# Expert outputs of an AdaLN attention + MoE block: six stored rows per token against four accumulator rows added by the scatter

## The chip, the core and the metric

The kernel runs on one core of a Trainium2 chip, in one launch. The metric is the device time in microseconds from the first to the last instruction of the core. Everything is float32 unless said otherwise. Engines are called PE (matrix multiply; PEld is its weight load), DVE (vector), ACT (scalar), POOL (GpSimd) and SP (the queue that issues most transfers).

## The reference

One transformer block on `x` of shape (8, 256, 256): adaptive layer norm, gated linear attention with ternary weights, residual, a second adaptive layer norm, and then a mixture of experts with a shared expert. Only the last part touches the change:

```python
# 2048 tokens, E = 64 experts, TOPK = 6 per token, H = 256, F = 96
pos  = position of the (token, expert) choice within its expert
valid = pos < CAP                       # CAP = 48 places per expert
buf[expert, pos] = h[token]             # choices past CAP are dropped
out  = (silu(buf @ w_gate) * (buf @ w_up)) @ w_down      # per expert
y[token] = sum over its valid choices of out[expert, pos] * weight
x = x + gb * (y + shared(h))
```

Of 12288 choices at most 64 x 48 = 3072 are valid; the others add nothing to `y`.

## The kernel before

**Token stage.** For each of 8 batches (256 tokens, two tiles of 128) the five engines run a software pipeline, `step(s, ...)` under `token_steps`: norms, attention, router, shared expert. Its result per batch is `pre` (residual plus gated shared expert, kept in SBUF) and a dispatch: POOL scatters each token's row, with its 64 expert weights and some keys, by `slot_ix` to memory (`rows_dram`, 64 experts x 64 slots, L449), 12 indirect transfers a batch. Beside it ACT issues one transfer per batch that fills an eighth of `y_dram` with zeros (L578), since most of its 12288 rows (six per token) are never written.

**Pair stage.** The 64 experts go two at a time, 32 pairs, under `pair_steps`. A pair is 128 slot rows: SP loads the rows of two pairs per transfer (L346) and, for pairs 0 to 15, behind them the weights of two later pairs (`load_quad`, L321 to L323; pairs 0 to 15 had theirs loaded in the token stage). PE transposes the rows (L1257), multiplies gate and up (L1268), transposes (L1275) and multiplies down (L1281). ACT does the tanh (L625), a copy, and the weighted evacuation of the down product into one of OBUF = 4 buffers `e_out` (the halves of `oT` and `osq`; L545 with `wcol`). DVE copies the transposed rows (L984), does the two products (L989, L992), copies the pair's weights (L1001), and works out for each slot row its place in `y_dram`: token times 6 plus the rank of this expert among the token's (`larger`, `rank`, `y_row`; L1003 to L1008). POOL then scatters the 128 rows by `y_row` to `y_dram` (`put`, L494), 1 KB a row; rows of empty slots get an index out of bounds and are left out.

After scatter q POOL waits for the landing of scatter q-3 and then raises `e_free` (L500), which ACT waits for ahead of an evacuation into a used buffer. So up to four scatters are under way.

**Last stage.** When all scatters have landed, SP reads `y_dram` in 16 tiles of 128 tokens, six rows (6 KB) per token (L366), through YBUF = 4 buffers. DVE sums six rows by a reduction (L1019); POOL multiplies by the gate `gb_all` (L516) and adds `pre` (L521), each behind a tiny `settle` instruction (L439); SP stores the tile (L370).

## Time and profile before

| | |
|---|---|
| median of 3 runs | 516.87 us (515.25 to 517.76) |
| profiled execution, first to last instruction | 517.1 us |
| token stage, about | 0 to 374 us |
| pair stage | 374 to 464 us |
| last stage | 464 to 517 us |
| busy over the span | PE 60%, DVE 55%, POOL 41%, ACT 19% |

The profiled execution is as long as the timed ones, so nothing lies around its span that a sum would have to add. The busy shares are averages over three stages with different limits: PE does nothing in the last 53 us, and DVE and POOL little in the pair stage. What the change does has to be read stage by stage.

### The profile page before, as it was taken

How to read it: one execution, taken by the hardware profiler on the slowest of the kernel's cores; microseconds unless marked ns; L12 is line 12 of the kernel's file. 1: busy time of each engine (PE TensorE's matmuls, PEld its weight loads, DVE VectorE, ACT ScalarE, POOL GpSimd, SP SyncE). 2: the span in 40 equal slices, each digit the busy share in tenths (PEclk: the TensorE clock that was granted, in tenths of full speed). 3: DMA queues.
4: the chain of work that ended last, by engine and by line, in shares of the span. 5: the costliest groups of instructions: out<-in, count | busy, mean ns of one | idle time of the engine just before them, and what ended most of it. 6: DMA issues, size and time to landing. Idle time of an engine off the chain costs nothing.

```text
span 517.1 us, 7330 instructions
## 1 busy us (share of the span) xinstructions
PE 309.6 (60%) x2282; PEld 222.4 (43%) x2282; DVE 283.7 (55%) x1066; ACT 98.9 (19%) x253; POOL 212.8 (41%) x310
## 2 busy tenths in 40 slices
PE   0735695968678768859657867150089889940000
PEld 0424484856556556747445655040045444520000
DVE  3550516395194394393393392664067544727995
ACT  1411131413112212303113201000024332430000
POOL 4200112117517527327327237186615433553664
PEclk9958568896786886796787787655579865985555
DMA  7955992963411311311301300000059999119992
GB/s 224 399 183 178 260 317 71 239 214 127 171 35 61 125 47 47 122 41 39 122 20 38 122 22 8 0 5 2 3 153 300 277 270 228 57 38 379 333 323 96
DMA packets 62332, 73.63 MB, mean 142 GB/s; under 512 B 9458, under 2 KB 56955, under 8 KB 62304
## 3 DMA queue, kind: packets, MB, share of 16 engines
q1 hardware_dynamic: 41456, 53.37, 35.2%
q10 hardware_dynamic: 14704, 15.24, 8.4%
q0 software_dynamic: 6144, 4.66, 3.1%
q8 instruction: 15, 0.25, 0.2%
q14 instruction: 13, 0.11, 0.1%
HBM read 48.39 MB, written 40.93 MB: 173 GB/s over the span
## 4 chain that ended last, share of the span: by engine, by line
issue 27%; PE 19%; DVE 16%; POOL 15%; DMA 10%; another core or an unknown queue 5%; ACT 3%; SPq 2%; DVEq 1%; ACTq 0%; POOLq 0%
POOL rows_dram L449 8%; PE ps_s L1268 5%; DVE z L1019 4%; DMA h2row<-rows_dram 2%; DVE scm L821 2%; DMA xa<-in_L_attn_x 2%; DMA scm<-rows_dram 2%; DMA egu<-y_dram 2%; POOL rstd L435 2%; PE ps_o L1166 2%; SPq L300 1%; PE ps_o L1281 1%; PE ps_a L1257 1%; PE ps_c L1281 1%
## 5 line engine op out<-in xcount | busy, mean ns | idle before, releaser
L449 POOL DMA_INDIRECT rows_dram<-h2row,slot_ix x96 | 94.3, 983 | 28.1 <-issue 28.1
L435 POOL TENSOR_TENSOR rstd<-ve,half_exp 128x2 f32<-128x2 f32 x15 | 11.2, 743 | 133.6 <-DVE ve L662 133.4
L1019 DVE TENSOR_REDUCE z<-egu 128x256 f32<-128x1536 f32 x16 | 42.7, 2746 | 10.8 <-DMA egu<-y_dram 10.8
L439 POOL TENSOR_TENSOR pool_pad<-half_exp 128x1 f32<-128x1 f32 x72 | 13.7, 191 | 68.4 <-ACT oT L545 17.0
L821 DVE TENSOR_TENSOR scm<-ps_s,decay 128x2048 f32<-128x2048 f32 x16 | 36.6, 2285 | 4.9 <-PE ps_s L1146 4.9
L1268 PE MATMUL ps_s<-egu,attn 128*64 128x192 f32 x256 | 33.7, 391 | 0.1
L1078 PE MATMUL ps_a<-hT,w_qkv 128*128 128x256 f32 x64 | 24.6, 551 | 11.9 <-ACT hsq L569 7.1
L1174 PE MATMUL ps_a<-ident,h2row 128*128 128x128 f32 x32 | 8.9, 435 | 36.7 <-POOL h2row L473 36.7
L1166 PE MATMUL ps_o<-scm,v_eo 128*32 128x128 f32 x512 | 26.8, 357 | 5.6 <-DVE scm L821 5.6
L827 DVE TENSOR_SCALAR r_den<-r_exp 128x128 f32<-128x128 f32 x8 | 1.8, 230 | 44.0 <-issue 35.0
L545 ACT ACTIVATE h2T<-ps_a 128x512 f32<-128x512 f32 x8 | 4.8, 597 | 105.5 <-PE ps_a L1174 105.5
L1078 PEld LDWEIGHTS ps_a<-hT,w_qkv 128*128 128x128 f32 x64 | 16.9, 278 | 15.7 <-issue 12.4
L1268 PEld LDWEIGHTS ps_s<-egu,attn 128*64 128x64 f32 x256 | 18.7, 158 | 7.7 <-issue 2.5
L1174 PEld LDWEIGHTS ps_a<-ident,h2row 128*128 128x128 f32 x32 | 5.7, 217 | 37.7 <-POOL h2row L473 37.7
L1129 PE MATMUL ps_c<-w_proj,oT 128*128 128x256 f32 x64 | 17.2, 415 | 7.4 <-issue 3.8
L1166 PEld LDWEIGHTS ps_o<-scm,v_eo 128*32 128x32 f32 x512 | 16.8, 138 | 11.1 <-issue 10.4
L1193 PE MATMUL ps_c<-h2T,ws_gu 128*96 128x256 f32 x64 | 21.4, 495 | 0.0
L625 ACT ACTIVATE z<-ps_s 128x96 f32<-128x96 f32 x32 | 8.0, 251 | 66.3 <-PE ps_s L1268 63.1
L1101 PE MATMUL ps_c<-w_qkv,hT 128*128 128x256 f32 x64 | 20.6, 480 | 0.0
L1146 PE MATMUL ps_s<-qT,k_eo 32*128 32x128 f32 x512 | 20.2, 297 | 0.0
L1257 PE MATMUL ps_a<-ident,h2row 128*128 128x128 f32 x16 | 4.6, 377 | 25.8 <-DMA h2row<-rows_dram 25.8
L494 POOL DMA_INDIRECT y_dram<-oT,y_row x16 | 15.9, 994 | 9.3 <-POOL pool_pad L439 5.1
(212 smaller groups left out, 725.3 us busy)
## 6 DMA issues: line engine op xcount, KB each, us to landing
y_dram<-y_zeros ACTq DMA_DIRECT2D x8, 1536.0 KB
egu<-y_dram SPq DMA_DIRECT2D x16, 768.0 KB, 5.9
egu<-in_L_ffn_w_gate SPq DMA_DIRECT2D x16, 384.0 KB, 6.7
egu<-in_L_ffn_w_up SPq DMA_DIRECT2D x16, 384.0 KB, 7.9
ed<-in_L_ffn_w_down SPq DMA_DIRECT2D x16, 384.0 KB, 9.7
rows_dram<-scm SPq DMA_DIRECT2D x1, 5376.0 KB, 15.8
mod_b<-mod_dram SPq DMA_DIRECT2D x8, 384.0 KB
h2row<-rows_dram SPq DMA_DIRECT2D x8, 336.0 KB
```

Source lines behind the costliest of these rows:

```text
L435: g.tensor_tensor(out_, in_, half_exp[:, which], ALU.pow).then_inc(S[done], 1)
L449: g.indirect_dma_start(out=rows_dram, out_offset=bass.IndirectOffsetOnAxis(ap=slot_ix[par][:, tile, j:j + 1], axis=0), in_=h2row[par][:, t ...
L494: g.indirect_dma_start(out=y_dram, out_offset=bass.IndirectOffsetOnAxis(ap=y_row[w][:, 0:1], axis=0), in_=e_out[n], in_offset=None, bounds ...
L821: v.tensor_tensor(scm[:].rearrange("p r j q t -> p (r j q t)"), ps_s[:].rearrange("p r n -> p (r n)"), decay[:].rearrange("p r j q t -> p ...
L1019: v.tensor_reduce(ysum[m % NT], y_in[m].rearrange("p (j c) -> p c j", c=C), AX_X, ALU.add).then_inc(S["y_sum"], 1)
L1078: last = mm.matmul(ps_a[:, N * j:N * j + N], w_qkv[:, k, P * j:P * j + P], hT[:, k], start=(k == 0), stop=(k == KC - 1))
L1101: last = mm.matmul(ps_c[:, C * i:C * i + C], hT[:, k, T * i:T * i + T], w_qkv[:, k, 2 * C:3 * C], start=(k == 0), stop=(k == KC - 1))
L1129: last = mm.matmul(ps_c[:, C * i:C * i + C], oT[:, i, k], w_proj[:, k], start=(k == 0), stop=(k == KC - 1))
L1146: last = mm.matmul(ps_s[:, r, col:col + T], k_eo[q][32 * r:32 * r + 32, j, ts], qT[32 * r:32 * r + 32, j, ts], start=True, stop=True)
L1166: last = mm.matmul(dst[32 * r:32 * r + 32], vq, scm[:, r, j, q], start=(q == 0 and not tile), stop=(q == 1), skip_group_check=True)
L1193: last = mm.matmul(ps_c[0:F, N * g_:N * g_ + N], ws_gu[:, k, g_], h2T[:, k], start=(k == 0), stop=(k == KC - 1))
L1268: last = mm.matmul(e_gups[n][rows].rearrange("p (g f) -> p g f", f=F), xt[n][:, k, rows], egu[:, slot // 2, :, 2 * (slot % 2) + half, k], ...
```

## The change

`y_dram` becomes two arrays (`TURNS = 2`) of 2 x 2048 token rows each, plus 128 spare rows. Pair q scatters into array q mod 2; its first expert into that array's first 2048 rows, its second expert into the other 2048 (`side_base`). So the rows of one scatter never meet, and the scatter adds to memory (`compute_op=ALU.add`) in place of writing. A token now has four rows to sum. The place of a row is its token number plus an offset, one DVE instruction in place of three, and the eight keys from which the rank was worked out go: a slot row is 324 numbers in place of 336. Rows of empty slots go to the 128 spare rows (the minimum with `no_token`), one for each partition.

Two scatters into one array could meet in a row, so scatter q is issued only when scatter q-2 has landed.

The last stage is rebuilt: no ring of buffers, all eight batches have their own place in SBUF (six in `egu`, one each in `scm` and `decay`), 32 loads of 256 KB are issued at once, for even batches by SP and for odd ones by ACT. DVE does all arithmetic, four instructions a batch; POOL has no part. Each batch is stored whole.

```diff
-TKEY = KEYS + 8
-ROWW = 336
-YROWS = B * N * TOPK
+TKEY = KEYS
+ROWW = 324
+TOKENS = B * N
+TURNS = 2
+SIDES = 2 * TURNS
+YROWS = 2 * TOKENS
+FAR = 16384
...
-        y_dram = nc.dram_tensor("y_dram", [YROWS, C], F32, kind="Internal").ap()
+        y_dram = [nc.dram_tensor(f"y_dram{i}", [YROWS + P, C], F32, kind="Internal").ap() for i in range(TURNS)]
...
-            for t in range(YBUF):
-                load_y(t, t)
-            with sp.Fori(0, B * NT // YBUF - 1) as i:
-                for m in range(YBUF):
-                    sp.wait_ge(S["y_sum"], YBUF * i + (m + 1))
-                    load_y(YBUF * i + (m + YBUF), m)
-                    store_out(YBUF * i + m, m % NT)
...
+            for b in range(0, B, 2):
+                for a in range(SIDES):
+                    sp.dma_start(y_in[b][:, a], y_v[a // 2][a % 2, b]).then_inc(S[f"ld_y{b}"], 16)
+            for b in range(B):
+                sp.wait_ge(S["y_out"], b + 1)
+                sp.dma_start(out_t[b], y_in[b][:, 0]).then_inc(S["st_out"], 16)
...
+            def put(q):
+                n = q % OBUF
                 pool.wait_ge(S["put_row"], q + 1)
                 pool.wait_ge(S["e_evac"], q + 1)
                 seen(pool, S["put_step"], q)
                 settle(2).then_inc(S["put_step"], 1)
...
-                    pool.wait_ge(S[f"st_put{(n + 1) % OBUF}"], last_n)
+                before_it = q - TURNS
+                if before_it >= 0:
+                    pool.wait_ge(S[f"st_put{before_it % OBUF}"], 16 * (before_it // OBUF + 1))
                     pool.sem_inc(S["e_free"], 1)
...
+                g.indirect_dma_start(out=y_dram[q % TURNS], out_offset=bass.IndirectOffsetOnAxis(ap=y_row[q % WBUF][:, 0:1], axis=0),
+                                     in_=e_out[n], in_offset=None, bounds_check=last_y, oob_is_err=True,
+                                     compute_op=ALU.add).then_inc(S[f"st_put{n}"], 16)
...
-                    a.dma_start(fill_v[s], spread(y_zeros[:], 1, N * TOPK // P)).then_inc(S["st_fill"], 16)
+                    for i in range(TURNS):
+                        a.dma_start(fill_v[i][s], spread(y_zeros[:], 1, 2 * N // P)).then_inc(S["st_fill"], 16)
...
+            def load_y():
+
+                for n in range(OBUF):
+                    act.wait_ge(S[f"st_put{n}"], 16 * PAIRS // OBUF)
+                for b in range(1, B, 2):
+                    for i in range(SIDES):
+                        a.dma_start(y_in[b][:, i], y_v[i // 2][i % 2, b]).then_inc(S[f"ld_y{b}"], 16)
...
-                    v.tensor_tensor(larger[:], xr[x][:, KEYS:TKEY], spread(slot_key[:, q + 1], 1, 8),
-                                    ALU.is_gt).then_inc(S["wcol_ready"], 1)
...
+                    v.tensor_scalar(y_row[w][:], xr[x][:, TKEY:TKEY + 1], side_base[:, 0:1], no_token[:, 0:1],
+                                    ALU.add, ALU.min).then_inc(S["put_row"], 1)
...
+            for b in range(B):
+                dve.wait_ge(S[f"ld_y{b}"], 16 * SIDES)
+                v.tensor_tensor(y_in[b][:, 0:2], y_in[b][:, 0:2], y_in[b][:, 2:4], ALU.add).then_inc(S["y_sum"], 1)
+                dve.wait_ge(S["y_sum"], 2 * b + 1)
+                v.tensor_tensor(y_in[b][:, 0], y_in[b][:, 0], y_in[b][:, 1], ALU.add).then_inc(S["y_sum"], 1)
+                dve.wait_ge(S["y_sum"], 2 * b + 2)
+                v.tensor_tensor(y_in[b][:, 0], y_in[b][:, 0], spread(gb_all[:, b], 1, NT), ALU.mult).then_inc(S["y_gb"], 1)
+                dve.wait_ge(S["y_gb"], b + 1)
+                v.tensor_tensor(y_in[b][:, 0], y_in[b][:, 0], pre[:, NT * b:NT * b + NT], ALU.add).then_inc(S["y_out"], 1)
```

POOL's instructions in the middle of the pair stage, before: a row is line, operation, names, shape, and the semaphores that it waits for. `st_put0` to `st_put3` count the landings of the scatters by buffer.

```order
L439 TENSOR_TENSOR pool_pad<-half_exp 128x1 [waits put_step,e_evac,put_row]
L494 DMA y_dram<-oT,y_row 12288x256
L490 REGISTER_ALU [waits st_put1]
L439 TENSOR_TENSOR pool_pad<-half_exp 128x1 [waits put_step,e_evac,put_row]
L494 DMA y_dram<-oT,y_row 12288x256
L490 REGISTER_ALU [waits st_put2]
```

The same place in the changed kernel, the first four scatters:

```order
L431 TENSOR_TENSOR pool_pad<-half_exp 128x1 [waits e_evac,put_row,st_fill]
L492 DMA y_dram<-oT,y_row 4224x256
L431 TENSOR_TENSOR pool_pad<-half_exp 128x1 [waits put_step,e_evac,put_row]
L492 DMA y_dram<-oT,y_row 4224x256
L431 TENSOR_TENSOR pool_pad<-half_exp 128x1 [waits put_step,e_evac,put_row]
L492 DMA y_dram<-osq,y_row 4224x256 [waits st_put0]
L431 TENSOR_TENSOR pool_pad<-half_exp 128x1 [waits put_step,e_evac,put_row]
L492 DMA y_dram<-osq,y_row 4224x256 [waits st_put1]
```

The wait for a landing has moved from behind a scatter, where it named the scatter three before, to ahead of it, where it names the scatter two before.

DVE's last stage before is a loop of reductions over four buffers:

```order
L1018 ISA [waits ld_y0]
L1019 TENSOR_REDUCE z<-egu 128x256 [waits y_gb]
L1018 REGISTER_ALU [waits ld_y1]
L1019 TENSOR_REDUCE z<-egu 128x256 [waits y_gb]
L1018 REGISTER_ALU [waits ld_y2]
L1019 TENSOR_REDUCE z<-egu 128x256 [waits y_gb]
```

After, two of the eight batches, written out:

```order
L993 TENSOR_TENSOR egu<-egu 128x1024 [waits ld_y5]
L995 TENSOR_TENSOR egu<-egu 128x512 [waits y_sum]
L997 TENSOR_TENSOR egu<-egu,gb_all 128x512 [waits y_sum]
L999 TENSOR_TENSOR egu<-egu,pre 128x512 [waits y_gb]
L993 TENSOR_TENSOR scm<-scm 128x1024 [waits ld_y6]
L995 TENSOR_TENSOR scm<-scm 128x512 [waits y_sum]
L997 TENSOR_TENSOR scm<-scm,gb_all 128x512 [waits y_sum]
L999 TENSOR_TENSOR scm<-scm,pre 128x512 [waits y_gb]
```

Gate and residual have moved from POOL to DVE, and no instruction waits for a buffer to come free.

## Rows read from the trace of the kernel before

**Rows 1.** The page: span, and PE and DMA share in 40 slices (tenths).

```profile
span 517.1 us, 7330 instructions
...
PE   0735695968678768859657867150089889940000
...
DMA  7955992963411311311301300000059999119992
```

**Rows 2.** Busy time by stage: PE, PEld, DVE, ACT, POOL, clock, DMA share, GB/s.

```profile
34.00:100.00 66.00, 47.64 (x406) 38.57 (x406) 26.50 (x82) 13.85 (x33) 7.32 (x9) 0.73 0.80 218
100.00:300.00 200.00, 148.28 (x1172) 119.04 (x1170) 113.11 (x504) 41.04 (x93) 88.11 (x97) 0.78 0.28 90
385.00:400.00 15.00, 15.00 (x110) 8.14 (x109) 11.30 (x59) 7.08 (x23) 8.19 (x14) 1.00 0.97 258
400.00:418.00 18.00, 14.17 (x92) 7.22 (x90) 10.49 (x54) 6.34 (x19) 8.26 (x14) 0.91 1.11 275
418.00:437.00 19.00, 18.40 (x79) 8.10 (x79) 8.13 (x40) 4.99 (x15) 5.74 (x9) 0.51 1.10 265
437.00:464.00 27.00, 21.91 (x156) 11.73 (x155) 14.56 (x74) 10.92 (x33) 15.38 (x26) 0.94 0.16 54
464.00:517.00 53.00, 0.00 (x0) 0.00 (x0) 42.75 (x16) 0.00 (x0) 27.67 (x64) 0.50 0.78 277
```

**Rows 3.** Groups by line, last stage: busy us, mean ns, idle before.

```profile
L1019 DVE TENSOR_REDUCE z<-egu 128x256 f32<-128x1536 f32 x16 | 42.7, 2746 | 10.8 <-DMA egu<-y_dram 10.8
L516 POOL TENSOR_TENSOR h2s<-z,gb_all 128x256 f32<-128x256 f32 x16 | 11.6, 725 | 0.0
```

**Rows 4.** Chain that ended last, around 464 us: start, us, what.

```profile
461.68 2.37 DMA y_dram<-osq,y_row
464.13 4.17 DMA egu<-y_dram
```

**Rows 5.** Timeline of POOL's last instruction: start, us.

```profile
512.51 0.72 POOL L521 TENSOR_TENSOR z<-h2s,pre 128x256 f32<-128x256 f32 x1
```

**Rows 6.** Timeline, pair stage: PE gate/up products, and ACT and POOL for one pair.

```profile
422.78 1.56 PE L1268 MATMUL ps_s<-egu,attn 128*64 128x192 f32 x8
426.33 1.55 PE L1268 MATMUL ps_s<-egu,attn 128*64 128x192 f32 x8
...
448.14 0.88 PE L1268 MATMUL ps_s<-egu,attn 128*64 128x192 f32 x8
...
449.89 0.47 ACT L545 ACTIVATE oT<-ps_o,wcol 128x256 f32<-128x256 f32 x1 [0.32 <-PE ps_o L1281]
...
450.21 0.88 PE L1268 MATMUL ps_s<-egu,attn 128*64 128x192 f32 x8
...
451.17 0.99 POOL L494 DMA_INDIRECT y_dram<-oT,y_row  x1 [0.48 <-POOL pool_pad L439]
```

**Rows 7.** Timeline: scatters 0, 2, 4, 7, 16; one evacuation of ACT.

```profile
384.95 0.99 POOL L494 DMA_INDIRECT y_dram<-oT,y_row  x1 [0.51 <-POOL pool_pad L439]
...
389.35 0.99 POOL L494 DMA_INDIRECT y_dram<-osq,y_row  x1 [0.49 <-issue]
...
393.16 0.99 POOL L494 DMA_INDIRECT y_dram<-oT,y_row  x1 [0.48 <-issue]
...
400.23 0.99 POOL L494 DMA_INDIRECT y_dram<-osq,y_row  x1 [0.48 <-DMA y_dram<-oT,y_row]
400.35 0.47 ACT L545 ACTIVATE oT<-ps_c,wcol 128x256 f32<-128x256 f32 x1 [0.51 <-POOLq L500]
...
427.10 0.99 POOL L494 DMA_INDIRECT y_dram<-oT,y_row  x1 [0.48 <-POOL pool_pad L439]
```

**Rows 8.** DMA in the window 390 to 435 us: queues and one kind of issue.

```profile
q1 hardware_dynamic: 12732, 11.40, 103.9%
q0 software_dynamic: 768, 0.83, 6.8%
...
egu<-in_L_ffn_w_up SPq DMA_DIRECT2D x7, 384.0 KB, 9.1
```

**Rows 9.** Groups by line, DVE: two sizes of a two-operand instruction.

```profile
L821 DVE TENSOR_TENSOR scm<-ps_s,decay 128x2048 f32<-128x2048 f32 x16 | 36.6, 2285 | 4.9 <-PE ps_s L1146 4.9
...
L810 DVE TENSOR_TENSOR x<-attn,xres 128x512 f32<-128x512 f32 x8 | 5.5, 692 | 0.7
```

**Rows 10.** The page: a DMA queue, and issues with KB each and us to landing.

```profile
q10 hardware_dynamic: 14704, 15.24, 8.4%
...
y_dram<-y_zeros ACTq DMA_DIRECT2D x8, 1536.0 KB
...
xa<-in_L_attn_x SPq DMA_DIRECT2D x8, 256.0 KB, 2.7
```

More of the change, by code:

```diff
@@ L241, in adaln_attention_moe @@
         xt_taken wcol_ready gup ge_exp gh_ready htp ht_taken dnp e_evac settled put_step put_row
-        rank_step y_sum y_gb y_out
-        """.split() + [f"ld_quad{i}" for i in range(QUADS)]
+        y_sum y_gb y_out
+        """.split() + [f"ld_quad{i}" for i in range(QUADS)] + [f"ld_y{b}" for b in range(B)]
         S = {n: sem(n) for n in names}
@@ L253, in adaln_attention_moe @@
         rows_v = rows_dram.rearrange("(r n p) c -> r p n c", p=P, n=2)
-        fill_v = y_dram.rearrange("(b p r) c -> b p (r c)", b=B, p=P).rearrange("b p (a n) -> b p a n", n=C)
-        y_v = y_dram.rearrange("(t p j) c -> t p (j c)", p=P, j=TOPK)
+        fill_v = [y[0:YROWS].rearrange("(b p r) c -> b p (r c)", b=B, p=P).rearrange("b p (a n) -> b p a n", n=C)
+                  for y in y_dram]
+        y_v = [y[0:YROWS].rearrange("(a b i p) c -> a b p i c", a=2, b=B, p=P) for y in y_dram]
         def token_steps(eng, step):
@@ L502, in _ @@
-            for q in range(OBUF - 1):
-                put(q, q, q, None)
-            turns = (PAIRS - OBUF) // WBUF
-            with pool.Fori(0, turns) as i:
-                for m in range(OBUF - 1, OBUF - 1 + WBUF):
-                    put(WBUF * i + m, m % OBUF, m % WBUF, 16 * (WBUF // OBUF * i + (m + 1) // OBUF))
-            for q in range(WBUF * turns + OBUF - 1, PAIRS):
-                put(q, q % OBUF, q % WBUF, 16 * ((q + 1) // OBUF))
-            def gate(t, b, i):
-                pool.wait_ge(S["y_sum"], t + 1)
-                pool.wait_ge(S["settled"], 2 * t + 1)
-                settle(4).then_inc(S["settled"], 1)
-                g.tensor_tensor(ygb[i], ysum[i], gb_all[:, b], ALU.mult).then_inc(S["y_gb"], 1)
-                pool.wait_ge(S["y_gb"], t + (NT + 1))
-                pool.wait_ge(S[f"st_y{i}"], 16 * b + 16)
-                pool.wait_ge(S["settled"], 2 * t + 2)
-                settle(4).then_inc(S["settled"], 1)
-                g.tensor_tensor(yout[i], ygb[i], pre[:, t], ALU.add).then_inc(S["y_out"], 1)
@@ L523, in _ @@
-            for i in range(NT):
-                pool.sem_inc(S[f"st_y{i}"], 16)
-            pool.sem_inc(S["settled"], 1)
-            pool.sem_inc(S["y_gb"], NT)
-            with pool.Fori(0, B) as b:
-                for i in range(NT):
-                    gate(NT * b + i, b, i)
+                before_it = q - TURNS
+                if before_it >= 0:
+                    pool.wait_ge(S[f"st_put{before_it % OBUF}"], 16 * (before_it // OBUF + 1))
+                    pool.sem_inc(S["e_free"], 1)
@@ L532, in _ @@
+                g.indirect_dma_start(out=y_dram[q % TURNS], out_offset=bass.IndirectOffsetOnAxis(ap=y_row[q % WBUF][:, 0:1], axis=0),
+                                     in_=e_out[n], in_offset=None, bounds_check=last_y, oob_is_err=True,
+                                     compute_op=ALU.add).then_inc(S[f"st_put{n}"], 16)
+            for q in range(PAIRS):
+                put(q)
         @block.scalar
@@ L614, in step @@
                     a.activation(s_exp[:], ps_c[0:F, 0:N], ACT.Tanh, scale=0.5).then_inc(S["sg_exp"], 1)
+            act.wait_ge(S["c_fill"], 1)
+            for y in y_dram:
+                a.dma_start(y[YROWS:YROWS + P], y_zeros[:]).then_inc(S["st_fill"], 16)
             norm1_out(0, 0)
             act.wait_ge(S["c_misc"], 1)
-            act.wait_ge(S["c_fill"], 1)
             token_steps(act, step)
+            def load_y():
[4 more added lines that the diff above has]
+                        a.dma_start(y_in[b][:, i], y_v[i // 2][i % 2, b]).then_inc(S[f"ld_y{b}"], 16)
             def pair_step(q, i, m):
@@ L703, in _ @@
             v.memset(ones_bf[:], 1.0)
+            for half in range(2):
+                v.memset(side_base[SLOTS * half:SLOTS * half + SLOTS], float(FAR + half * TOKENS))
             v.tensor_scalar(part_bit[:], part_ix[:], HD, None, ALU.bitwise_and).then_inc(S["prologue_step"], 1)
@@ L931, in slots @@
                 for i in range(NT):
-                    last = v.max(h2row[par][:, i, KEYS:TKEY], key[:, i])
+                    last = v.max(top_key[:, i], key[:, i])
                 last.then_inc(S["slot_step"], 1)
```

65 lines of the change are left out of this document (20 added, 45 removed).

## The prediction, made before the changed kernel had run

> **What bounds the kernel now.** I read the slices of the page first. PE's share and that of the DMA engines change character several times [rows 1], so a busy share over the span of 517.1 us says nothing here; the sum is made stage by stage, against the profiled execution's 517.1 us, which is 0.2 us from the median of the runs (516.87).
>
> Then the busy time by stage [rows 2]. From 464 to 517 us PE and ACT do nothing. DVE is busy for 42.75 of 53 us with 16 reductions of 2746 ns and idle for 10.8 us, of which nearly all is the first wait for `y_dram` [rows 3]. The last stage is DVE's: POOL's gate takes 725 ns a tile and hides beside it, and the transfers keep up (share 0.78). It opens with the last scatter, 2.37 us from issue to landing, and the first load of 768 KB, 4.17 us [rows 4], and closes with POOL's last addition, which ends at 513.2, 3.9 us before the end: the last store and its landing [rows 5].
>
> The pair stage has two halves. From 437 us on the DMA engines are nearly idle (0.16), PE has the full clock, and a pair takes 2.07 us, from one gate/up product to the next (448.14, 450.21) [rows 2, 6]. From 385 to 437 us the DMA share is 0.97 to 1.11 [rows 2]: weights and slot rows for later pairs. Scatters 0 to 16 take from 384.95 to 427.10 [rows 7], 2.63 us a pair, and after 418 PE is at the lower level of its clock (1.2 GHz, 0.51 granted) after a stretch in which it had gaps; there a pair takes 3.55 us (422.78, 426.33) [rows 6].
>
> **The landing of a scatter** is the number on which the change rests, and there are two. Quiet: 2.37 us [rows 4]. In the loaded stretch: ACT's evacuation at 400.35 was released by POOL's `e_free`, raised for the landing of scatter 4, and the trace puts a landing of a scatter out of `oT` in the 0.48 us ahead of 400.23 [rows 7]. Scatter 4 was issued at 393.16, so it took 6.6 to 7.1 us; I take 6.6. That fits its surroundings: a 384 KB load took 9.1 us there [rows 8]. Before, four scatters may be under way, so 6.6 us allows one each 1.7 us and costs nothing. After, only two may.
>
> **1. The scatter in pairs 0 to 16: the chain of landings becomes the bound.** An adding scatter must fetch its 128 destination rows as well, and the rows of empty slots are now moved too. No row shows an adding transfer. Nearest are packets of 1 KB on queue 10: 8.4% of 16 engines x 517.1 us over 14704 packets is 47 ns each [rows 10], so 128 rows on 16 engines take 0.38 us, and a read beside the write makes it 0.75. The scatters of the loaded stretch used 6.8% of 45 us x 16 engines for 17 scatters, 0.18 us each [rows 8]. Lower bound of the change in landing: nothing (the read hides in the queueing). Upper bound: the read queues as long again as the write did, 4.2 us (6.6 less 2.37). I take 0.75, nearer the lower end, because in the quiet stretch most of the 2.37 us isn't data. That gives 7.35 loaded and 3.1 quiet. With 0.1 us to wake, scatter q follows scatter q-2 by 7.45 us: a period of 3.73 us against 2.63.
>
> Scatter 2 can still go at 389.35 [rows 7]; scatter 16 then goes at 389.35 + 14 x 3.73 = 441.5, against 427.10. Queued behind a waiting scatter on POOL is only the next one; but `e_free` is raised there, so ACT's evacuations, and through them PE, keep two pairs ahead of the scatter and no more. The loads: two pairs bring about 1.5 MB, 5.6 us at the 270 GB/s of this stretch [rows 2], and the scatters add up to 2 x 0.57; 6.8 us of 7.5. So the engines stay loaded, and the long landing persists until the weights are in, near scatter 16. The same loads that held PE up before no longer do: they have slack in a 3.73 us pair.
>
> **2. Pairs 17 to 31.** 2 x 2.07 = 4.14 us between a scatter and the last but one covers 3.1 + 0.1. PE sets the pace again. When scatter 16 goes, evacuation 18 is free: evacuation 31 starts 13 x 2.07 = 26.9 us later, its scatter 1.28 us behind (449.89 to 451.17 [rows 6]), its landing 3.1 us behind that: 441.5 + 26.9 + 1.3 + 3.1 = 472.8, against 464.05. The stage costs 8.8 us. This has PE at the full clock after 441; before, PE lost time at the lower one between 418 and 437, and that is part of what this sum gets back.
>
> **3. DVE's two instructions fewer per pair** are worth nothing: PE sets the 2.07 us, and DVE is busy 14.56 of 27 us there [rows 2].
>
> **4. The last stage.** Loads: 8.4 MB in 8192 rows of 1 KB in place of 12.6 MB in rows of 6 KB. The batches 0 and 1 come together, one from each queue: 2048 x 47 ns / 16 = 6.0 us, plus what a small load takes beyond its data (xa: 2.7 us for 256 packets, 0.75 of it data [rows 10]), 1.9: 7.9 us. DVE per batch: the sizes 2048 and 512 took 2285 and 692 ns [rows 9], 1.04 ns an element, so 1024 elements take 1.22 us; with three of 692 ns and some 0.15 us between them, 3.45 us a batch. By DVE batches 6 and 7 could start at 7.9 + 6 x 3.45 = 28.6. By DMA they have landed after 8192 packets and the stores of five batches (1280): 9472 x 47 / 16 = 27.8, plus 1.9: 29.7. Then 6.9 us of DVE and the 3.9 us of the last store: 40.5 us against 53.1, a gain of 12.6. Bounds: 39.4 (DVE alone), and 48.2 if reads run at the 270 GB/s of the loaded stretch (9.7 MB: 35.5 us). I take 40.5, since these are even rows without a second kind of traffic.
>
> **5. The rest.** Fills shrink from 12.6 to 8.7 MB (eight of 1536 KB before [rows 10]). From 100 us on the DMA share is 0.28 and nothing waits for them; before 100 it is 0.80 [rows 2], and two or three fills of 0.5 MB less, 1.5 us each at 47 ns a KB, could give up to 4 us. Slot rows are 4% shorter. I take 0.5 us off. ACT issues one more transfer per batch, beside 74% idle.
>
> **Sum:** 472.8 + 40.5 - 0.5 = 512.8 us.
>
> One rule speaks against the change. By the Trainium skill, "Collectives: The Full Stack", section "The bandwidth ceiling", an adding transfer reads two sources through the same ring and runs at about half the rate of a copy. No row here shows an adding transfer; by that rule the data of a scatter would double, as the 0.75 us does from its own rows, and the sum would stay 512.8.
>
> **The rivals.**
>
> *A. The adding scatter lands much later (slower).* Place: POOL's wait ahead of the scatter, pairs 2 to 16. The point from which it decides: the stage may cost 12.6 + 0.5 us, so scatter 16 at 445.8, a period of 4.03, a loaded landing of 8.0 us, 1.4 more than a plain one. At a period of 4.6 (landing 9.1, halfway to the upper bound of 10.8) scatter 16 goes at 453.8 and the end is at 525. For it: a read ahead of each write under a loaded queue. Against: slower pairs relieve the queue. Chance 0.23.
>
> *B. PE's clock.* A period of 3.73 us leaves PE a third idle at full speed. If it is at the lower level for the first 20 us after 441, as for 19 us before, 5.6 pairs at 3.55 cost 8.3 us: 521. For it: gaps came before the fall at 418. Against: at 3.55 us a pair PE has no gaps, and at 437 it was back. Chance 0.10.
>
> *C. Reads of 1 KB rows from two queues at 270 GB/s.* The last stage takes 48.2: 520.5; between this and the forecast lie results within 0.5% of before. Chance 0.17, most of it in that middle.
>
> *D. The chain of landings is no bound:* with half as many scatters queued each lands sooner, in 5 us or less, a period of 2.6, and the pair stage costs 1 us or so: 505. For it: a landing of 6.6 includes queueing. Against: the queue is filled by loads, 103.9% against 6.8% [rows 8]. Chance 0.12.
>
> *Forecast,* 507 to 517: 0.38.
>
> **Numbers.** A measurement tells 0.5% (2.6 us) from no change. Faster: D, three quarters of the forecast (0.29), 0.01 of C: 0.42. Same: the rest of the forecast and 0.13 of C: 0.22. Slower: A, B, the rest of C: 0.36. The range 504 to 526 leaves out the far ends of A and D.
>
> **What would show it.** Step 1: POOL idle ahead of the scatter in pairs 2 to 16 with a landing as releaser, scatters 3.7 us apart, PE no longer waiting for slot rows. Step 2: 2.07 us a pair from scatter 18 on, last landing near 473. Step 4: first DVE addition 8 us after the last landing, DVE's 32 instructions 27.6 us in all. The prediction is wrong if a quiet landing exceeds 4.1 us (then the second half stretches too), or if the loaded one is under 5 or over 8 us.

## The result and the profile after

| | before | after |
|---|---|---|
| median of 4 runs | 517.32 us (515.25 to 521.2) | 530.93 us (529.22 to 536.25) |
| profiled execution, span | 517.1 us | 527.9 us |
| first scatter issued | 384.95 | 388.32 |
| last scatter landed | 464.05 | 490.36 |
| last stage, from there to the end | 53.1 us | 37.5 us |

The change makes the kernel slower: the ratio is 1.0254, with an interval of 1.0159 to 1.0349. The forecast was 512.8 us, and 526 was the upper end of its range. The last stage gave back more than forecast (15.6 us against 12.6). The last landing came 26.3 us later where 8.8 had been allowed: the pair stage began 3.4 us later and lasted 22.9 us longer.

The forecast was a sum over the span of the profile, and was taken to hold for the timed executions as it stood. It doesn't quite: the profiled execution of the changed kernel was timed at 529.72 us and its span is 527.9, so 1.8 us lie around the span. Of the 18.1 us between forecast and median, 15.1 lie in the span and are accounted for below. Medians here are of all executions, but ratios leave out those that fell into a slower state of the chip, so the two can differ.

The page of the changed kernel answers to [rows 1] and [rows 10]: the span, PE and DMA in 40 slices, POOL's scatters of either source, the packets of POOL's queue, and the small loads of the last stage.

```profile
span 527.9 us, 6983 instructions
...
PE   0744795959657864957957766150198789981000
...
DMA  7939992944211220220210210000359997545895
...
q0 software_dynamic: 9216, 6.76, 8.0%
...
L492 POOL DMA_INDIRECT y_dram<-osq,y_row x16 | 24.9, 1555 | 22.6 <-ACT oT L513 18.2
...
egu<-y_dram SPq DMA_DIRECT2D x12, 256.0 KB, 9.3
```

The busy time by stage answers to [rows 2] (PE, PEld, DVE, ACT, POOL, clock, DMA share, GB/s):

```profile
385.00:400.00 15.00, 15.00 (x112) 8.36 (x112) 10.25 (x48) 6.66 (x22) 7.07 (x9) 1.00 0.80 209
400.00:418.00 18.00, 14.06 (x71) 6.45 (x69) 5.55 (x25) 3.09 (x12) 7.42 (x10) 0.63 1.13 289
418.00:437.00 19.00, 15.97 (x68) 6.84 (x66) 5.38 (x24) 3.50 (x13) 7.16 (x8) 0.50 0.95 221
437.00:464.00 27.00, 26.91 (x141) 12.76 (x139) 12.68 (x57) 8.30 (x30) 16.61 (x19) 0.65 0.70 137
464.00:475.00 11.00, 9.13 (x69) 4.75 (x65) 6.04 (x29) 3.86 (x15) 8.69 (x11) 1.00 0.48 52
...
490.00:528.00 38.00, 0.00 (x0) 0.00 (x0) 25.78 (x32) 0.00 (x0) 0.00 (x0) 0.50 0.86 276
```

From 400 to 437 us PE did 139 matrix products where it did 171 before, with DMA shares of 1.13 and 0.95 in place of 1.11 and 1.10. From 418 on the DMA share falls (0.95, then 0.70, then 0.48), and the loads no longer hold anything up: from the first scatter on PE waited 4.5 us for slot rows before, and never for a load now.

The chain that ended last says what does (start, us, what). Before, it went through PE and loads and met one scatter, the last [rows 4]. Now:

```profile
388.32 5.70 DMA y_dram<-oT,y_row
394.06 0.56 issue
394.84 8.55 DMA y_dram<-osq,y_row
403.55 0.48 ACT osq L513
404.19 8.14 DMA y_dram<-oT,y_row
...
413.13 8.38 DMA y_dram<-osq,y_row
...
451.39 1.58 issue
453.18 4.88 DMA y_dram<-oT,y_row
...
463.44 3.86 DMA y_dram<-oT,y_row
467.46 0.48 ACT oT L513
468.10 3.77 DMA y_dram<-osq,y_row
...
486.55 3.81 DMA y_dram<-osq,y_row
...
491.89 6.86 DMA egu<-y_dram
498.77 1.24 DVE egu L993
```

This is a chain of sixteen scatters, mostly every second one. Their landings sum to 85.8 of the 102.0 us between 388.32 and 490.36. Three things are to be read here. First, the landing: 8.1 to 8.6 us for the three scatters of the chain issued between 394 and 414, 3.7 to 3.9 from 458 on, and values between these in the middle.

Second, from a landing to the next start there are 0.8 us: 394.02 to 394.84, 403.39 to 404.19, 467.30 to 468.10. An evacuation by ACT stands in some of these gaps, but it is not what the scatter waits for. The one at 403.55 belongs to scatter 6, while scatter 4, which starts at 404.19, had its data at 395.69; the same landing released both. The first gap, from 394.02, has no evacuation and is as long.

Third, three gaps between 429 and 453 are longer (2.75, 2.74 and 1.84 us). Two of them are made by the chain's going over from the even scatters to the odd ones. Scatter 10 starts 0.80 us after the landing at 429.69, and scatter 11 follows 1.95 us behind, with POOL's own work between:

```profile
430.49 1.56 POOL L492 DMA_INDIRECT y_dram<-osq,y_row  x1 [3.80 <-ACT oT L513]
431.55 0.73 POOL L431 TENSOR_TENSOR pool_pad<-half_exp 128x1 f32<-128x1 f32 x1
432.44 1.56 POOL L492 DMA_INDIRECT y_dram<-osq,y_row  x1 [0.16 <-POOL pool_pad L431]
...
437.34 1.55 POOL L492 DMA_INDIRECT y_dram<-oT,y_row  x1 [3.12 <-DMA y_dram<-osq,y_row]
```

It is the same at 444.83 and 446.77. By the program scatter 12 waits for scatter 10, whose landing the trace has at 436.55, again 0.8 us ahead of 437.34. Of the third gap, before scatter 17 at 453.18, 1.0 us stays unexplained.

PE, which is busy for 26.91 of 27 us at a granted 0.65 from 437 to 464, is in none of these gaps. POOL's small `settle` instruction stands behind the waits for the evacuation and for the row numbers, and it waited once, ahead of the first scatter (engine, line, what it waited for, us, times, longest):

```profile
POOL pool_pad L431 <- DVE y_row L985: 11.6, 1, 11.6
```

Each scatter from the fourth on found its evacuation finished 4.7 to 10.2 us before, where it was 0.8 to 2.9 us in the kernel before. So the profile's label "ACT" in POOL's idle time is a coincidence in time, and the forecast's rival B (PE's clock) had no part in the chain.

The queue of POOL in a quiet stretch of 12 to 14 us, before with seven scatters and after with six (packets, MB, share of 16 engines):

```profile
q0 software_dynamic: 336, 0.43, 10.7%
```

```profile
q0 software_dynamic: 872, 0.79, 51.8%
```

Before (452 to 464 us) that is 0.107 x 12 / 7 = 0.18 us of all 16 engines per scatter; after (476 to 490) it is 0.518 x 14 / 6 = 1.21 us. The packets changed too: the scatters of before moved their 1943 rows (filled slots only) in 495 packets, nearly all of 4 KB, at 178 ns each; those of after are 4096 packets of 1 KB, one for each slot row, at 102 ns (medians over the pair stage).

The last stage, to set beside [rows 3], and the store that ends it:

```profile
L993 DVE TENSOR_TENSOR egu<-egu 128x1024 f32<-128x1024 f32 x6 | 7.3, 1220 | 23.6 <-DMA egu<-y_dram 23.6
L999 DVE TENSOR_TENSOR egu<-egu,pre 128x512 f32<-128x512 f32 x6 | 4.2, 692 | 0.2
```

```profile
525.39 0.37 SPq L373 DMA_DIRECT2D out<-decay  x1
```

DVE waits once, for the first batch, and never again; then eight batches follow each other every 3.32 us from 498.77 on.

### The profile page after: what moved, and what is told of

Its sections match the earlier page's. It is cut to its first block, busy times and chain, and to the rows that moved or that the text cites. A ratio compares the mean times of both kernels' runs of the same rounds, so it can differ in the third digit from the quotient of the medians.

```text
span 527.9 us, 6983 instructions
## 1 busy us (share of the span) xinstructions
PE 321.1 (61%) x2282; PEld 225.9 (43%) x2282; DVE 260.5 (49%) x1020; ACT 95.2 (18%) x253; POOL 204.6 (39%) x246
## 4 chain that ended last, share of the span: by engine, by line
issue 25%; DMA 22%; DVE 20%; PE 11%; POOL 10%; another core or an unknown queue 6%; ACT 2%; SPq 2%; ACTq 0%; POOLq 0%; DVEq 0%
DMA y_dram<-oT,y_row 8%; DMA y_dram<-osq,y_row 8%; POOL rows_dram L441 4%; DVE scm L803 2%; PE ps_o L1145 2%; DMA xa<-in_L_attn_x 2%; POOL rstd L427 2%; PE ps_a L1057 1%; SPq L303 1%; DVE egu L993 1%; DMA egu<-y_dram 1%; POOL h2row L465 1%; POOL h2s L461 1%; PE ps_a L1153 1%
## 5 line engine op out<-in xcount | busy, mean ns | idle before, releaser
L1057 PE MATMUL ps_a<-hT,w_qkv 128*128 128x256 f32 x64 | 26.4, 584 | 21.0 <-issue 10.0
L1247 PE MATMUL ps_s<-egu,attn 128*64 128x192 f32 x256 | 37.9, 431 | 0.1
L492 POOL DMA_INDIRECT y_dram<-osq,y_row x16 | 24.9, 1555 | 22.6 <-ACT oT L513 18.2
L492 POOL DMA_INDIRECT y_dram<-oT,y_row x16 | 25.0, 1561 | 20.7 <-ACT osq L513 13.7
L431 POOL TENSOR_TENSOR pool_pad<-half_exp 128x1 f32<-128x1 f32 x40 | 23.4, 584 | 21.2 <-DVE y_row L985 11.6
L971 DVE SCALAR_TENSOR_TENSOR z<-z,ps_s 128x96 f32<-128x96 f32 x32 | 8.1, 254 | 46.5 <-ACT z L604 45.7
L1057 PEld LDWEIGHTS ps_a<-hT,w_qkv 128*128 128x128 f32 x64 | 18.0, 295 | 25.2 <-issue 21.5
L1247 PEld LDWEIGHTS ps_s<-egu,attn 128*64 128x64 f32 x256 | 20.5, 174 | 9.7 <-issue 4.4
L1108 PE MATMUL ps_c<-w_proj,oT 128*128 128x256 f32 x64 | 17.6, 422 | 8.1 <-issue 4.2
L1172 PE MATMUL ps_c<-h2T,ws_gu 128*96 128x256 f32 x64 | 22.5, 515 | 0.0
L1064 PE MATMUL ps_b<-hT,w_qkv 128*128 128x256 f32 x64 | 19.3, 456 | 0.0
```

Source lines behind the costliest of these rows:

```text
L431: return g.tensor_tensor(pool_pad[:, at:at + 1], half_exp[:, 0, 0:1], half_exp[:, 0, 0:1], ALU.add)
L492: g.indirect_dma_start(out=y_dram[q % TURNS], out_offset=bass.IndirectOffsetOnAxis(ap=y_row[q % WBUF][:, 0:1], axis=0), in_=e_out[n], in_o ...
L1057: last = mm.matmul(ps_a[:, N * j:N * j + N], w_qkv[:, k, P * j:P * j + P], hT[:, k], start=(k == 0), stop=(k == KC - 1))
L1064: last = mm.matmul(ps_b[:, N * j:N * j + N], w_qkv[:, k, C + P * j:C + P * j + P], hT[:, k], start=(k == 0), stop=(k == KC - 1))
L1172: last = mm.matmul(ps_c[0:F, N * g_:N * g_ + N], ws_gu[:, k, g_], h2T[:, k], start=(k == 0), stop=(k == KC - 1))
L1247: last = mm.matmul(e_gups[n][rows].rearrange("p (g f) -> p g f", f=F), xt[n][:, k, rows], egu[:, slot // 2, :, 2 * (slot % 2) + half, k], ...
```

## The experiments

They ran in three groups, each on a chip of its own. The kernel before took a median of 474.65 us there in the first group (472.27 to 479.56), 475.58 in the second (470.75 to 484.58) and 473.9 in the third (472.64 to 483.77), some 43 us less than in the comparison above; its first scatter went at 335.07 us in the one trace of it there, 49.9 us earlier. So the token stage was shorter there; why is open (the mean granted clock of that trace is 0.79, that of the kernel before in the first comparison 0.74). Every ratio below is to the kernel before of the same group. "Pair stage" is here from the first scatter's issue to the end of the last scatter's last packet, 0.3 us ahead of its landing; in the first comparison it went from 78.8 to 101.7 us. The "last stage" of these runs begins there too.

Theory ADD x WAIT: an adding scatter lands later, and only two may be under way; neither costs much by itself, both together do (in the expectations of the first four runs "Theory ADD" stands for this, later ADD x WAIT). The rivals: WAIT (two under way is the cost, whatever the scatter does), ADD (the addition alone), ROWS (the rows of empty slots, now moved as well).

**b_wait2.** The kernel before, its loop of scatters written out, with the changed kernel's wait and still without addition:

```
+                before_it = q - 2
+                if before_it >= 0:
+                    pool.wait_ge(S[f"st_put{before_it % OBUF}"], 16 * (before_it // OBUF + 1))
+                    pool.sem_inc(S["e_free"], 1)
                 g.indirect_dma_start(out=y_dram, ...)
-                if last_n is not None:
-                    pool.wait_ge(S[f"st_put{(n + 1) % OBUF}"], last_n)
-                    pool.sem_inc(S["e_free"], 1)
```

> The kernel before with one thing changed: scatter q waits, ahead of its issue, for the landing of scatter q-2 (POOL's scatters written out, not looped). Plain writes, six rows per token, empty slots left out. Theory ADD (the added read in the scatter makes it land late, and two at a time make that the bound): a plain scatter lands 6.6 us after its issue in the loaded stretch and 2.1 to 2.4 in the quiet one, with 0.8 us from landing to the next issue as in the changed kernel, so 3.7 us a pair up to scatter 16 and 2.07 after: scatter 16 near 441, last landing near 470, some 522 us, 1% over before. Theory WAIT (the wait for the last but one is the whole cost, whatever the transfer does): last landing near 487, 540 us (the changed kernel's pair stage with the old last stage). Theory ROWS (rows of empty slots): as ADD, no loss or little.

Measured: 480.0 us, ratio 1.0116 (1.0048 to 1.0183). The profiled execution is the longest of the five (486.77 us); its pair stage takes 91.5 us, with the granted clock at 0.50 from 370 to 415, so this length says little about the wait.

**b_add.** The kernel before with four scatters under way, each of them adding, the loop again written out:

```
-                                     oob_is_err=False).then_inc(S[f"st_put{n}"], 16)
+                                     oob_is_err=False, compute_op=ALU.add).then_inc(S[f"st_put{n}"], 16)
```

> The kernel before with the scatter adding to memory in place of writing (each row is still its own, so each gets zero plus its value), four under way as before. Theory ADD: loaded landing 8.2 us in place of 6.6 and quiet 3.8 in place of 2.4, hidden by four under way; 517 to 520 us, unless POOL's part of the issue grows from 0.99 to 1.56 us, still hidden in 2.07 us. Theory WAIT: the same. Theory ROWS: POOL's part stays 0.99 us, since empty slots stay out, and landings stay at 6.6 and 2.4.

Measured: 481.48 us, ratio 1.0129 (1.0032 to 1.0227). No loss was expected. Pair stage 88.1 us. POOL's scatter takes 1.55 us here too, though empty slots are still dropped: that length belongs to the addition.

**b_add_wait2.** Both edits.

> Both: the scatter adds and waits for the last but one; empty slots left out. Theory ADD: the pair stage of the changed kernel: scatters 4.6 us apart under load and 2.33 us apart after, last landing near 487 and 540 us. Theory ROWS: half of the scatter's rows are missing, so landings near the plain ones, and the time of the first of these kernels, some 522 us. Theory WAIT: 540 us, and the first of these kernels as well.

Measured: 495.25 us, ratio 1.044 (1.0372 to 1.0508). Pair stage 99.1 us. The two single effects add up to 1.0245; together they cost nearly twice that. WAIT and ADD each fall as the whole cause. No kernel had its loop of scatters written out and nothing else changed, so what that alone does to the three ratios is not known.

**a_plain.** The changed kernel with writes in place of additions, so that its sums are left out; two under way, all rows moved:

```
-                                     in_=e_out[n], in_offset=None, bounds_check=last_y, oob_is_err=True,
-                                     compute_op=ALU.add).then_inc(S[f"st_put{n}"], 16)
+                                     in_=e_out[n], in_offset=None, bounds_check=last_y, oob_is_err=True).then_inc(S[f"st_put{n}"], 16)
```

> The changed kernel with plain writes in place of additions (so a token keeps only the last of several outputs in one array), all 128 rows moved, still behind the landing of the last but one. Theory ADD: landings fall from 8.2 to 6.6 and from 3.8 to 2.4 us, the pair stage ends 10 to 14 us sooner, and the total is 515 to 520. Theory ROWS: landings stay near 8 and 3.5 us, and the total stays near 530. Theory WAIT: 530, or as far under it as one finds the wait to cost less for a shorter landing.

Measured: 466.85 us, ratio 0.984 (0.9746 to 0.9934), below the 515 to 520 us that were expected beside 517 for the kernel before. Pair stage 85.6 us, against 101.7 with the addition. The chain of its trace:

```profile
338.35 6.43 DMA y_dram<-oT,y_row
345.58 7.18 DMA y_dram<-osq,y_row
353.57 6.94 DMA y_dram<-oT,y_row
361.32 7.33 DMA y_dram<-osq,y_row
```

It is the same chain of landings with the same 0.8 us between them (344.78 to 345.58), but the loaded ones are 6.9 to 7.5 us where they were 8.1 to 8.6 with the addition, and it lets go of the kernel once the loads are in: from scatter 16 to the last it takes 28.5 us, where the changed kernel takes 37.1. So the wait with plain writes is affordable, and the new last stage is worth more than it.

**after_again** and **after_third.** The changed kernel itself, beside the groups that follow.

> The changed kernel as it stands, timed beside the next three on one chip. ADD x WAIT (an adding scatter lands later, and only two are under way, so the two costs multiply): the pair stage, from the first scatter's issue to the last landing, is 99 to 102 us in place of 79 to 80, the last stage 37.5 in place of 53, so 1.015 to 1.03 times the kernel before. The rival, that the token stage costs a part of it too, has the first scatter 3 us or more later than in the kernel before.

Measured: 480.92 us, ratio 1.0104 (1.0 to 1.0209), below the 1.015 to 1.03 expected. Pair stage 100.6 us, last stage 37.6.

> The changed kernel again, beside the kernel before and the next two. ADD x WAIT with the clock's part as above: pair stage 99 to 102 us, last stage 37.5, the time 1.005 to 1.025 of the kernel before.

Measured: 481.75 us, ratio 1.0162 (1.0095 to 1.0228). Pair stage 101.3 us. The stages of the change are as long here as in the first comparison; the ratio is smaller. The first scatter goes at 340.2 us in both of these traces; in b_sum and b_last, which are the kernel before up to there, it goes at 341.3 and 339.2.

**a_drop.** The changed kernel with `last_y` at the last real row and `oob_is_err=False`, so that rows of empty slots are dropped.

> The changed kernel, with the rows of empty slots dropped by the bound (some 1940 rows moved of 4096). ROWS (the rows of empty slots, which the change sends along, are what lengthens a landing): the loaded landing falls by 1 us or more, the pair stage to 92 us or less, and the time below that of the changed kernel by 2%. ADD x WAIT: the pair stage stays at 99 to 101 us, and the time within 0.7% of the changed kernel's.

Measured: 478.76 us, ratio 1.0102 (1.0062 to 1.0141), 0.4% below the changed kernel of the same group, with 1943 data packets in place of 4096. Pair stage 98.2 us. ROWS falls: it is 2 to 3 us.

**a_four.** The changed kernel with four arrays and so four adding scatters under way; the last stage reads the first two arrays alone, which leaves half the pairs out of the sum:

```
-                before_it = q - TURNS
+                g.indirect_dma_start(out=(y_dram + y_more)[q % OBUF], ...
+                                     compute_op=ALU.add).then_inc(S[f"st_put{n}"], 16)
+                before_it = q - (OBUF - 1)
```

> The changed kernel with four arrays instead of two, so that four adding scatters are under way as before; the last stage reads the first two arrays alone, so half the pairs are left out of the sum, with reads and additions as many as in the changed kernel. ADD x WAIT: the pair stage falls from 100 to 88 us (as with the addition alone in the kernel before), POOL's adding scatters still take 1.55 us and land 7 us after issue under load, and the time is 2.3 to 2.8% below the changed kernel's, near 0.985 of the kernel before. If the addition alone were the cost, the pair stage would stay within 3 us of the changed kernel's and the time within 0.7%.

Measured: 469.17 us, ratio 0.9801 (0.9659 to 0.9942), 2.4% below the changed kernel. Pair stage 88.3 us. Its chain has no scatter but the last; PE's products and a load for it are back:

```profile
364.67 1.49 PE ps_s L1248 x8
...
383.75 11.74 DMA scm<-rows_dram
...
427.33 3.79 DMA y_more<-osq,y_row
```

POOL's 1.56 us per adding scatter and loaded landings (7.0 to 8.9 us) are all still there. They cost nothing that can be told from PE's own pace once four are under way.

**a_three.** The changed kernel with three accumulators, six rows per token read and added at the end.

> The changed kernel with three accumulators in place of two: six rows per token read at the end (in two batches of additions as in the run before this one), and three adding scatters under way. ADD x WAIT: with a loaded landing of 7 to 8 us and 0.8 us to the next issue, three under way allow one each 2.9 us, near what PE and the loads allow, so most of the pair stage's cost is gone: 89 to 93 us. The last stage reads as much as that of the kernel before: 44 to 47 us. The time is 0.985 to 1.005 of the kernel before. If the number under way doesn't matter, the pair stage stays at 99 us or more and the time is 1.01 or above.

Measured: 479.82 us, ratio 1.0137 (1.0062 to 1.0212). The pair stage is short, 86.4 us, below the 89 to 93 expected: the third scatter under way already undoes the cost. The total was missed because of the last stage: 52.6 us, not 44 to 47. Batches 0 and 1 are asked for together from two queues, 3 MB, so the first addition waits until 11.3 us after the last packet (434.40 against 423.07), and the eight batches then take 4.6 us each, with one wait of 1.9 us for a store among them.

```profile
434.40 1.76 DVE L1002 TENSOR_TENSOR egu<-egu 128x1536 f32<-128x1536 f32 x1 [20.41 <-DMA egu<-y_dram]
...
438.98 1.75 DVE L1002 TENSOR_TENSOR egu<-egu 128x1536 f32<-128x1536 f32 x1
```

**before_again.** The kernel before, traced once on such a chip.

> The kernel before, for a trace of it beside the next three on the same chip. CLOCK (where PE falls to the lower level early in the pair stage, the kernel before is held by PE at 3.6 us a pair, which no wait of the changed kernel makes worse, so the change costs less there): the pair stage takes 84 to 90 us in place of the 78.8 that it took on the chip of the first comparison, with some eight or more pairs at 3.5 to 3.6 us. The rival, that the pair stage of the kernel before is the same on every chip: 78 to 80 us, and the token stage holds the difference.

Measured: 466.53 us, a shorter execution than any of the seven timed ones; its pair stage takes 76.0 us, and the expectation of 84 to 90 failed for it. But b_sum and b_last below run the kernel before up to the last scatter, and their profiled executions (488.38 and 472.05 us, both among the longest of their kernels) took 89.3 and 84.9 us for the pair stage. The slices show the difference in PE's clock, first before_again, then b_sum:

```profile
385.00:411.00 26.00, 21.09 (x153) 11.11 (x149) 14.15 (x73) 10.90 (x33) 15.22 (x25) 0.96 0.23 75
```

```profile
400.00:415.00 15.00, 15.00 (x65) 6.40 (x63) 6.51 (x32) 4.11 (x13) 5.51 (x9) 0.50 0.06 22
```

In b_sum PE is busy without a pause at the lower level (0.50 granted), after a stretch from 385 to 400 with 11.43 us of 15 busy, and its scatters come every 3.6 us; in before_again they come every 2.1 us there. So the same pair stage of the kernel before varies by 13 us, and by these slices with the clock, while that of the changed kernel, held by landings, was 101.7, 100.6 and 101.3 us in its three traces. The runs say the same: beside one another, 19 runs of the kernel before spread over 13.8 us (470.75 to 484.58), four of the changed one over 2.1 (480.17 to 482.28) and ten of a_drop over 5.4 (476.78 to 482.17). The first comparison doesn't bear this out: four executions of either kernel spread over 6.0 us before and 7.0 after. The smaller ratios of the later groups fit it, but no pair stage of a typical execution of before was traced there, so it stays a guess.

**b_sum.** The kernel before with its reduction over six rows done as three additions:

```
-                    v.tensor_reduce(ysum[m % NT], y_in[m].rearrange("p (j c) -> p c j", c=C), AX_X,
-                                    ALU.add).then_inc(S["y_sum"], 1)
+                    v.tensor_tensor(yb[:, 0:3 * C], yb[:, 0:3 * C], yb[:, 3 * C:6 * C], ALU.add)...
+                    v.tensor_tensor(yb[:, 0:C], yb[:, 0:C], yb[:, C:2 * C], ALU.add)...
+                    v.tensor_tensor(ysum[m % NT], yb[:, 0:C], yb[:, 2 * C:3 * C], ALU.add)...
```

> The kernel before, scatters and all, with the one reduction over six rows per token done as three additions (768, 256 and 256 elements). What the changed kernel gains is in the last stage, where a reduction took 2746 ns for 1536 inputs and an addition of 1024 elements took 1.22 us. By these rows three additions are 0.95 + 0.4 + 0.4, 1.8 us a tile, so DVE needs 29 us instead of 43.9, and the transfers (12.6 MB and 2 MB out) set the stage: 40 to 44 us instead of 53, the pair stage unchanged, the time 0.972 to 0.982 of the kernel before. The rival, that these reads keep to the pace of 768 KB in 2.7 to 3 us that they had beside the reduction, leaves the stage at 48 us or more, 0.99.

Measured: 477.26 us, ratio 0.9986 (0.9921 to 1.0051), no difference; neither the expected 0.972 to 0.982 nor the rival's 0.99 came. The three additions take 1064 + 903 + 771 = 2738 ns, as long as the one reduction of 2746 ns [rows 3]. The timeline shows what lengthens them; first DVE, then POOL in the same two microseconds:

```profile
441.44 0.97 DVE L1022 TENSOR_TENSOR egu<-egu 128x256 f32<-128x256 f32 x1
442.45 0.99 DVE L1024 TENSOR_TENSOR z<-egu 128x256 f32<-128x256 f32 x1
...
445.35 0.43 DVE L1024 TENSOR_TENSOR z<-egu 128x256 f32<-128x256 f32 x1
```

```profile
441.41 0.72 POOL L516 TENSOR_TENSOR h2s<-z,gb_all 128x256 f32<-128x256 f32 x1
...
442.43 0.72 POOL L521 TENSOR_TENSOR z<-h2s,pre 128x256 f32<-128x256 f32 x1
```

An addition of 256 elements takes 0.43 us, and 0.97 to 0.99 when POOL's gate or addition starts within 0.03 us of it. Beside the reduction, POOL's gate ran for its 725 ns [rows 3] without lengthening it: the 16 reductions take 2733 to 2762 ns, the first of them with POOL still idle. The Trainium skill, "GPSIMD Engine Reference", section "1. Specifications", says that GpSimd and VectorE share their access to SBUF and contend when a DVE instruction has two inputs in SBUF; the trace agrees, at 0.97 against 0.43 us.

**b_last.** The kernel before up to its last scatter, and a last stage in the changed kernel's manner: two tiles at a time, everything on DVE, nothing on POOL (SP loads batch b + 4 behind the last read of batch b):

```
+                v.tensor_tensor(yb[:, :, 0:3 * C], yb[:, :, 0:3 * C], yb[:, :, 3 * C:6 * C], ALU.add)...
+                v.tensor_tensor(yb[:, :, 0:C], yb[:, :, 0:C], yb[:, :, C:2 * C], ALU.add)...
+                v.tensor_tensor(yo, yb[:, :, 0:C], yb[:, :, 2 * C:3 * C], ALU.add)...
+                v.tensor_tensor(yo, yo, spread(gb_all[:, b], 1, NT), ALU.mult)...
+                v.tensor_tensor(yo, yo, pre[:, NT * b:NT * b + NT], ALU.add)...
```

> The kernel before up to its last scatter (six rows per token, no addition in memory, four scatters under way); its last stage done as the changed kernel does it, two tiles at a time with every addition on DVE and nothing on POOL. By the changed kernel's rows (1024 elements 1.22 us, 512 elements 0.69 us) DVE needs 1.75 + 4 x 0.69 = 4.5 us for two tiles, 36 us in all; 14.7 MB at the 349 to 375 GB/s that this stage reached on this chip take 39 to 42. So 44 to 46 us for the stage in place of 53, and 0.980 to 0.988 of the kernel before. The rival, that additions in DVE are as slow here as they were beside POOL's gate (0.97 us for 256 elements), leaves the time within 0.5% of the kernel before.

Measured: 465.24 us (458.27 to 472.05, four executions), ratio 0.9717 (0.9608 to 0.9826). It beats both kernels. Its last stage takes 45.8 us as expected, DVE 35.6 us of it:

```profile
L992 DVE TENSOR_TENSOR egu<-egu 128x1536 f32<-128x1536 f32 x8 | 14.0, 1752 | 12.7 <-DMA egu<-y_dram 12.7
```

```profile
424.00:470.00 46.00, 0.00 (x0) 0.00 (x0) 35.59 (x40) 0.00 (x0) 0.00 (x0) 0.50 0.80 319
```

The stage explains 7 to 8 us. The medians differ by 8.7 us (473.9 against 465.24, 0.982), as expected. The ratio is worth 13, with an interval from 8 to 19, but it rests on two of the four executions, 458.27 and 463.23 us. So nothing beyond the stage is shown.

## Why the prediction was wrong

**The table of the pair stage**, from the runs: additions with two under way 98.2 to 101.7 us (five traces), additions with three or four 86.4 to 88.3 (three), writes with two 85.6 and 91.5, writes with four 76.0 to 89.3 (four). Only the first kind lies well outside what the kernel before spreads over; the 91.5 is 2.2 us beyond it, in an execution with PE at the lower clock for 45 us.

**Step 1, the loaded half.** The mechanism was right: POOL waits ahead of the scatter, and the chain of landings sets the pace. The sum has an error at its start: "Scatter 2 can still go at 389.35" is the time of the kernel before, but in the changed kernel scatter 2 waits for scatter 0 (`st_put0` in the listing of the change). It went 6.5 us after scatter 0 where the sum has 4.4. The landing was sized at 7.35 us and is 8.1 to 8.6 at first; the 0.1 us to wake is 0.8. The period is then (8.4 + 0.8) / 2 = 4.6 us and not 3.73, but only from scatter 2 to 8. The 0.1 was the delay to ACT's evacuation. POOL's own was in the rows: each scatter in [rows 7] has 0.48 us of idle time ahead of it, two of them put down to "issue". It cost nothing while the wait lay behind the scatter, and entered the chain when the wait moved ahead of it. The period didn't stay at 4.6: the landings shorten from 425 us on, when the loads have caught up, and from scatter 8 to 16 it is 3.4 us. Over the 14 scatters of the sum it is 3.90 us, near the 3.73 that was forecast, because a landing sized too short at first and too long later evened out; that is luck. Scatter 16 went at 449.5, not 441.5: 3.4 us of that were there at the first scatter, 2.1 come from the wait of scatter 2, and 2.5 from the period.

**The addition's size in step 1.** 0.75 us for 128 more reads came from packets of 47 ns. In the quiet stretch a scatter now occupies the 16 engines for 1.21 us instead of 0.18, and its landing went from 2.37 to 3.81: 1.44 us, twice what was taken. The rows of empty slots are a small part of this: a_plain writes all 128 rows and occupies the engines for 0.231 x 16 / 10 = 0.37 us a scatter (404 to 420 us), and its landings there are 2.4 us, but for one of 3.3. Of the 1.44 us, 0.56 may be POOL's longer issue (1.55 against 0.99), since a landing is counted from the issue's start; no run separates the two. The prediction's sentence on the Trainium skill, "Collectives: The Full Stack", gave no more than that 0.75; these runs put the whole price of the addition at about twice it. In time per byte the rule of half the rate comes near: 102 ns for an adding packet of 1 KB against 178 ns for a plain one of 4 KB is 2.3 times as long. The same skill's "DMA: Bandwidth & Descriptors", section "Anatomy of one DMA", says that most of the fixed time of such a transfer is the confirmation of the last write. No run here splits a landing into these parts.

**Step 2 is the step that failed most.** "2 x 2.07 = 4.14 us between a scatter and the last but one covers 3.1 + 0.1" is false with 3.8 + 0.8 = 4.6: the chain of landings holds to the end, at 2.3 us a pair from scatter 21 on, with PE at the full clock and idle in between (9.13 of 11 us busy, granted 1.00, from 464 to 475). The forecast had 28.2 us from scatter 16 to 31, since PE would have run ahead; they took 37.1, and 0.7 more for the last landing. Some 2.4 of these 8.9 us lie between scatters 16 and 19: the landings of 16 and 17 were still 4.8 to 4.9 us, and the unexplained 1.0 us stands there. Of the two tests that the prediction set itself, the loaded landing over 8 us did show the miss. The quiet landing above 4.1 us did not, for the same reason as the sum: it left out the 0.7 us of POOL's start.

So the miss of the pair stage, 490.4 - 472.8 = 17.6 us, is 3.4 (first scatter) + 2.1 (scatter 2) + 2.5 (to scatter 16) + 8.9 (to scatter 31) + 0.7. The first of these is not explained. First scatters went anywhere between 335.1 and 342.5 us in the later traces, with both kinds of kernel among the early and the late ones, so it is not taken for an effect of the change. That the addition and the wait cost most of this only together is shown by b_wait2, b_add, b_add_wait2, a_three and a_four. That the chain's 0.8 us is POOL's own is read from the traces with and without the addition; no kernel without it was run.

**Step 3** was not tested by itself; nothing speaks against it, since DVE held up no scatter but the first.

**Step 4** held in its mechanism and was 3.0 us too high. The first addition came 8.4 us after the landing (7.9 forecast), a batch takes 3.32 us (3.45), and the reads stayed ahead of DVE all the way, where they had been given 29.7 us for the batches 6 and 7. The stage is 37.5 us, below the bound of 39.4 by DVE alone, as a batch takes 0.13 us less and the last store's end 2.5 us in place of 3.9: DVE ends at 525.4 and the span at 527.9.

**Step 5**: 0.5 us off; the first scatter was 3.4 us later instead.

**The rivals.** A (23 in 100 against the forecast's 38) came nearest, with its place and mechanism and with its landing of 8.0 us passed. But its period of 4.6 us held only from scatter 2 to 8, and the 3.90 over the whole half is below the 4.03 from which it was to decide. What spoke against it, that slower pairs relieve the queue, came true from 425 us on. The larger part of the miss lies in pairs 17 to 31, which no rival priced. B did not happen: PE was at the lower clock after 437, yet no scatter waited for it (its own premise, PE "a third idle", should be 1.66 of 3.73 us, 45%). C did not (the reads kept ahead of DVE), and D did not: landings were 7.2 to 8.6 us from scatter 1 to 8.

## What to carry to other kernels

When a wait moves ahead of an instruction in a chain, the price per link is the landing plus the issuing engine's own start, which costs nothing while the wait stands behind; multiply by the links and compare with the slowest other engine at each end of the stage. An addition in memory brings such a chain where two scatters may meet in a row, so count how many may be under way: here two cost 10 to 15 us more than three or four, and three cost nothing that could be told from the clock's spread. A profile puts an idle time down to whatever ended just before it; check by the program which wait it was. And ask whether the gain needs the change at all: the cheaper last stage could be had without touching the scatters, and that version was the fastest.

## What was not expected of the hardware

- The adding scatter moved one packet of 1 KB per row (102 ns), the plain one packets of 4 KB (178 ns) for the same rows; POOL spent 1.55 us on issuing one against 0.99, with or without the empty rows.
- A plain and an adding scatter in a chain start 0.8 us after the landing that they wait for.
- A DVE addition of 256 elements takes 0.43 us alone and 0.97 beside POOL's; a DVE reduction beside the same POOL instructions is not lengthened.
- The pair stage of one and the same code varied from 76.0 to 89.3 us with the level of PE's granted clock.
